# Edge features multiplied as split fp32r halves on 128 rows, with ScalarE filling the banks of all edge pairs and b_e added on TensorE or in DRAM

## What is computed

```python
ea = edge_attr @ w_e + b_e                     # (E, 64) @ (64, 256)
msg = relu(x[src] + ea)                        # gathered rows of x
agg = segment_sum(msg, dst, N)                 # dst is sorted
t = x + agg
h_local = bn(relu(t @ w1 + b1) @ w2 + b2 + x)
h_attn = bn(attention(x) @ out_w.T + out_b + x)    # 4 heads, blocks of 32 nodes
out = h_local + h_attn
out = out + relu(out @ m_w1 + m_b1) @ m_w2 + m_b2
result = layernorm(x + bn(out))
```

## Time and profile before

| | |
|---|---|
| time, median of 3 runs | 1360.22 us (1359.91 to 1360.58) |
| the profiled execution, its own time | 1364.96 us |
| its span, first to last instruction | 1363.1 us |
| PE busy | 1270.4 us, 93% of the span |
| POOL busy | 987.6 us, 72% |
| DVE busy | 904.9 us, 66% |
| ACT busy | 751.6 us, 55% |
| mean granted TensorE clock | 0.979 of 2.4 GHz |

### The profile page before, as it was taken

The page is one execution under the profiler, slowest core; times in us unless marked ns, Lnnn a source line. Parts: engine busy times, 40 slices in busy tenths (PEclk is TensorE's granted clock), DMA queues, the critical chain, the costliest instruction groups (busy, mean ns, idle before and its releaser), DMA issues.

```text
span 1363.1 us, 22611 instructions
## 1 busy us (share of the span) xinstructions
PE 1270.4 (93%) x8250; PEld 1024.2 (75%) x8250; DVE 904.9 (66%) x1763; ACT 751.6 (55%) x1617; POOL 987.6 (72%) x1032
## 2 busy tenths in 40 slices
PE   3787889999999999999999999999999999999997
PEld 2666678887877777777778777777877777778786
DVE  4988987666666665667666566666666666556652
ACT  1333335665665656566665666666656656565642
POOL 7777777777777777777777777777777777777710
PEclk6889999999999999999999999999999999999999
DMA  9777765555555554555555555555555555545511
GB/s 328 236 242 244 243 212 157 172 151 164 160 174 174 160 174 139 174 161 176 174 159 163 148 166 170 174 164 172 149 161 160 175 177 160 172 131 167 153 52 47
DMA packets 109648, 232.89 MB, mean 171 GB/s; under 512 B 21984, under 2 KB 46816, under 8 KB 109536
## 3 DMA queue, kind: packets, MB, share of 16 engines
q0 software_dynamic: 49152, 134.28, 34.1%
q1 hardware_dynamic: 58944, 93.87, 20.6%
q10 hardware_dynamic: 1440, 3.29, 0.6%
HBM read 206.19 MB, written 25.17 MB: 170 GB/s over the span
## 4 chain that ended last, share of the span: by engine, by line
POOL 35%; PE 23%; DMA 15%; issue 13%; ACT 7%; DVE 6%; SPq 0%; DVEq 0%; ACTq 0%
POOL xg L304 35%; DMA xg<-xb_dram,srcs 12%; PE both L677 8%; PE bank L722 4%; PE bank L707 4%; ACT bank L330 3%; PE bank L677 3%; ACT mh L334 2%; DVE onehot L545 1%; DMA aggT<-in_xT_dram 1%; DVE ml L533 1%; PE bank L731 1%; PE both L853 1%; DMA xg<-in_x_dram,srcs 1%; PE bank L800 1%
## 5 line engine op out<-in xcount | busy, mean ns | idle before, releaser
L304 POOL DMA_INDIRECT xg<-xb_dram,srcs x864 | 819.3, 948 | 263.2 <-issue 227.0
L330 ACT COPY bank<-xg 128x512 f32<-128x512 f32 x432 | 256.3, 598 | 373.5 <-DMA xg<-xb_dram,srcs 341.7
L533 DVE SCALAR_TENSOR_TENSOR ml<-bank,mh 128x512 fp32r<-128x512 f32 x512 | 328.6, 683 | 154.6 <-ACT mh L334 153.6
L334 ACT ACTIVATE mh<-bank 128x512 fp32r<-128x512 f32 x512 | 276.7, 593 | 137.6 <-PE bank L707 136.4
L707 PE MATMUL bank<-we,ea 64*128 64x256 f32 x2048 | 296.1, 409 | 56.7 <-DVE bank L442 28.3
L707 PEld LDWEIGHTS bank<-we,ea 64*128 64x128 f32 x2048 | 181.7, 191 | 139.1 <-issue 68.3
L722 PE MATMUL bank<-mh,onehot 128*128 128x256 f32 x1024 | 265.8, 297 | 8.3 <-DVE onehot L545 8.2
L722 PE MATMUL bank<-ml,onehot 128*128 128x256 f32 x1024 | 252.3, 284 | 0.0
L722 PEld LDWEIGHTS bank<-mh,onehot 128*128 128x128 f32 x1024 | 196.4, 192 | 51.8 <-issue 29.5
L304 POOL DMA_INDIRECT xg<-in_x_dram,srcs x160 | 167.3, 1046 | 50.8 <-issue 46.9
L722 PEld LDWEIGHTS bank<-ml,onehot 128*128 128x128 f32 x1024 | 197.1, 192 | 0.0
(11 more groups left out here) (100 smaller groups left out, 1368.3 us busy)
## 6 DMA issues: line engine op xcount, KB each, us to landing
ea<-in_ea_dram SPq DMA_DIRECT2D x128, 256.0 KB, 5.0
xg<-xb_dram,srcs POOLq DMA_INDIRECT x864, 3.0
xT<-in_xT_dram SPq DMA_DIRECT2D x32, 256.0 KB, 3.2
aggT<-in_xT_dram SPq DMA_DIRECT2D x32, 256.0 KB, 3.9
xrow<-in_x_dram SPq DMA_DIRECT2D x16, 512.0 KB, 6.1
xb_dram<-xrow SPq DMA_DIRECT2D x16, 512.0 KB, 3.7
oT_dram<-oT SPq DMA_DIRECT2D x32, 256.0 KB, 2.3
xn<-in_x_dram SPq DMA_DIRECT2D x32, 256.0 KB, 4.5
```

Of the source, the lines that this page charges most:

```text
L304: pool.indirect_dma_start(xg[:, q % NX, n * C:(n + 1) * C], None, t["x"] if q < XB_PAIR else k.xb_dram[:, :], bass.IndirectOffsetOnAxis(k. ...
L330: nc.scalar.copy(EA[q % 4][:, :], xg[:, q % NX, :]).then_inc(s_seed, 1)
L334: nc.scalar.activation(mh[:, q % NM, :], EA[q % 4][:, :], ACT.Relu).then_inc(s_mh, 1)
L533: nc.vector.scalar_tensor_tensor(ml[:, q % NM, :], EA[q % 4][:, :], 0.0, mh[:, q % NM, :].bitcast(fp32), ALU.max, ALU.subtract).then_inc(s ...
```

## The change

- The edge product. w_e is split into a rounded fp32r part `weh` and a remainder `wel`. The edge features of each group are split too: ACT rounds the whole tile into a PSUM bank (`round_ea`) and writes the rounded halves to SBUF (`high_ea`, two copies of 64 partitions), DVE writes the remainders (`low_ea`, two tensor_tensor of 64 partitions, one operand in PSUM). They are stacked: the 64 high rows and the 64 low rows of a pair fill 128 partitions of `eahl`. A tile is now two fp32r matmuls of 128 rows, one by `weh`, one by `wel`.
- The seed. ACT copies the gathered rows into the banks of all pairs. For the first 80 pairs PE adds b_e by one more fp32r matmul per tile (`be_ones` x `be_hl`). DVE seeds no more.
- `XB` is 32 in place of 16: parts of 256 KB, one per turn in place of one per two turns, and `XB_PAIR` is 80 as before.
- `round_ea` for a later group stands on ACT in odd turns behind `high` and ahead of `copy_agg`; it uses the bank of the turn's first pair and so waits until DVE's `low` of that pair is done. `high_ea` stands behind `copy_agg`. `low_ea` stands on DVE behind the two `low` of odd turns. The seed that takes that bank next waits for `low_ea`.
- For room in SBUF: `ea` has 2 buffers in place of 3, `xn` one in place of two, `ex` and `prob` share the place of `dif`, and `we` and the gammas lie in tiles that are used later.

```diff
-NEA = 3
+NEA = 2
-XB = 16
+XB = 32
-XB_PAIR = XB * PG + 16
+XB_PAIR = 2 * XB + 16
...
             def load_ea(n):
                 if n >= NEA:
-                    sp.wait_ge(s_prod, 2 * (n - NEA) + 2)
+                    sp.wait_ge(s_eah, n - NEA + 1)
+                    sp.wait_ge(s_eal, n - NEA + 1)
...
-                m = turn // 2
-                if turn % 2 == 1 and m < XB:
+                m = turn
+                if m < XB:
                     sp.wait_ge(s_xadd, m + 1)
                     sp.dma_start(xb_parts[m, :, :, :], k.xrow[:, m % 2, :, :]
                                  ).then_inc(s_xbst[m % 2], 16)
-                if turn % 2 == 1 and 2 <= m + 1 < XB:
+                if 2 <= m + 1 < XB:
                     load_part(m + 1)
...
-                        if j >= 2:
-                            sp.wait_ge(s_r, j - 1)
-                        sp.dma_start(k.xn[:, j % 2, :, :], x_blocks[j, :, :, :]
+                        if j >= 1:
+                            sp.wait_ge(s_r, j)
+                        sp.dma_start(k.xn[:, 0, :, :], x_blocks[j, :, :, :]
...
             def seed(q):
                 act.wait_ge(s_xg[q % NX], 32 * (q // NX + 1))
-                act.wait_ge(s_ml, q - 3)
+                if q < 4:
+                    act.wait_ge(s_set, 1)
+                else:
+                    act.wait_ge(s_ml, q - 3)
+                if q % 4 == 2 and 6 <= q and q // 4 + 2 <= NG:
+                    act.wait_ge(s_eal, q // 4 + 2)
                 nc.scalar.copy(EA[q % 4][:, :], xg[:, q % NX, :]).then_inc(s_seed, 1)
...
+            def round_ea(n, bank):
+                act.wait_ge(s_ea[n % NEA], 16 * (n // NEA + 1))
+                nc.scalar.copy(bank[:, :].bitcast(f32r), ea[:, n % NEA, :]).then_inc(s_eab, 1)
+
+            def high_ea(n):
+                nc.scalar.copy(eahl[0:ED, n % 2, 0, :], ea[0:ED, n % NEA, :])
+                nc.scalar.copy(eahl[ED:P, n % 2, 1, :], ea[ED:P, n % NEA, :]).then_inc(s_eah, 1)
...
                 for q in (a, b):
                     if q < NP:
                         high(q)
+                n = (turn + 3) // 2
+                if turn % 2 == 1 and n < NG:
+                    act.wait_ge(s_ml, a + 1)
+                    round_ea(n, EA[a % 4])
                 if turn % 2 == 1 and 3 <= turn <= 2 * NG + 1:
                     copy_agg(turn // 2 - 1)
-                n = turn // 2 + 1
-                if turn % 2 == 0 and EA_PE <= n < NG:
-                    act.wait_ge(s_ea[n % NEA], 16 * (n // NEA + 1))
+                if turn % 2 == 1 and n < NG:
+                    high_ea(n)
...
+            def low_ea(n, bank):
+                dve.wait_ge(s_eab, n + 1)
+                nc.vector.tensor_tensor(eahl[ED:P, n % 2, 0, :], ea[0:ED, n % NEA, :],
+                                        bank[0:ED, :], ALU.subtract)
+                nc.vector.tensor_tensor(eahl[0:ED, n % 2, 1, :], ea[ED:P, n % NEA, :],
+                                        bank[ED:P, :], ALU.subtract).then_inc(s_eal, 1)
...
-                for q in (a + 2, b + 2):
-                    if q < XB_PAIR:
-                        seed(q)
                 n = turn // 2
                 if turn % 2 == 0 and n >= 1:
                     if 2 <= n < NG + 2:
                         add_agg(n - 2)
-                    if n < XB:
-                        add_be(n)
                     if n < NG:
                         make_onehot(n)
+                if 1 <= turn < XB:
+                    add_be(turn)
                 for q in (a, b):
                     if q < NP:
                         low(q)
+                if turn % 2 == 1 and (turn + 3) // 2 < NG:
+                    low_ea((turn + 3) // 2, EA[a % 4])
...
-                for two in range(2):
-                    for pair in range(2):
-                        rows = slice(pair * ED, (pair + 1) * ED)
+                pe.wait_ge(s_seed, 2 * d + 2)
+                for pair in range(2):
+                    for two in range(2):
                         at = (2 * h + two) * P
-                        ins = nc.tensor.matmul(EA[(2 * d + pair) % 4][:, two * C:(two + 1) * C],
-                                               ea[rows, n % NEA, at:at + P], k.we[rows, :],
-                                               start=False, stop=True,
-                                               skip_group_check=True)
+                        if 2 * d + pair < XB_PAIR:
+                            nc.tensor.matmul(EA[(2 * d + pair) % 4][:, two * C:(two + 1) * C],
+                                             k.be_ones[:, :], k.be_hl[:, :], start=False, stop=True,
+                                             skip_group_check=True)
+                        for half in (k.weh, k.wel):
+                            ins = nc.tensor.matmul(EA[(2 * d + pair) % 4][:, two * C:(two + 1) * C],
+                                                   eahl[:, n % 2, pair, at:at + P], half[:, :],
+                                                   start=False, stop=True, skip_group_check=True)
                 ins.then_inc(s_prod, 1)
```

More of the change, by code:

```diff
@@ L48 @@
 TURNS = LAST_START + NODE_TURNS
-EA_PE = XB_PAIR // PG + 1
 def nodes_in(turn):
@@ L95, in gnn_layer @@
         k.rel = sb("rel", [P, NG, TG])
-        k.we = sb("we", [P, C])
-        k.be_rows = sb("be_rows", [P, C])
+        k.weh, k.wel = sb("weh", [P, C], f32r), sb("wel", [P, C], f32r)
+        k.be_rows, k.be_hl = sb("be_rows", [P, C]), sb("be_hl", [P, C], f32r)
+        k.be_ones = sb("be_ones", [P, P], f32r)
         k.xrow = sb("xrow", [P, 2, XB_ROWS, C])
@@ L160, in program @@
         s_oh = sem("s_onehot_made")
+        s_weh, s_wel = sem("s_we_high"), sem("s_we_low")
+        s_eab, s_eah, s_eal = (sem(n) for n in ("s_ea_high_in_bank", "s_ea_high", "s_ea_low"))
         s_pre = [sem(f"s_agg_preloaded_{n}") for n in range(2)]
@@ L236, in _ @@
                 i, p = turn // TI, turn % TI
-                if turn % 2 == 1 and turn // 2 + 2 < NG:
-                    load_ea(turn // 2 + 2)
-                m = turn // 2
-                if turn % 2 == 1 and m < XB:
+                if turn == 0:
+                    load_ea(2)
+                if turn % 2 == 0 and turn // 2 + 3 < NG:
+                    load_ea(turn // 2 + 3)
+                m = turn
+                if m < XB:
                     sp.wait_ge(s_xadd, m + 1)
@@ L297, in _ @@
                         pool.wait_ge(s_xbst[n], 16 * (XB // 2))
[L298 to L301 removed]
+                if q >= NX:
+                    pool.wait_ge(s_seed, q - NX + 1)
                 for n in range(2):
@@ L401, in node @@
                                          ).then_inc(s_root, 1)
+            act.wait_ge(s_we, 16)
+            nc.scalar.copy(k.weh[:, :], k.we[:, :]).then_inc(s_weh, 1)
+            for n in range(2):
+                round_ea(n, X[1 + n])
+                high_ea(n)
+                if n == 0:
+                    seed(0)
+                    seed(1)
             for turn in range(TURNS):
@@ L405, in _ @@
                 for q in (a + 2, b + 2):
-                    if XB_PAIR <= q < NP:
+                    if q < NP:
                         seed(q)
@@ L453, in _ @@
             dve.wait_ge(s_ber, 16)
-            seed(0)
-            seed(1)
+            step_of(nc.vector.tensor_scalar(k.be_hl[:, :], k.be_rows[:, :], 0.0, None, ALU.mult))
+            settle()
+            for row in (0, 32):
+                nc.vector.tensor_scalar(k.be_ones[row:row + 1, :], ident[row:row + 1, :], 0.0, 1.0,
+                                        ALU.mult, ALU.add)
+            step_of(nc.vector.tensor_copy(k.be_hl[0:1, :], k.be_rows[0:1, :]))
+            settle()
+            nc.vector.tensor_tensor(k.be_hl[32:33, :], k.be_rows[0:1, :],
+                                    k.be_hl[0:1, :].bitcast(fp32), ALU.subtract).then_inc(s_be, 1)
+            dve.wait_ge(s_weh, 1)
+            nc.vector.tensor_tensor(k.wel[:, :], k.we[:, :], k.weh[:, :].bitcast(fp32),
+                                    ALU.subtract).then_inc(s_wel, 1)
+            low_ea(0, X[1])
             dve.wait_ge(s_dstg, 16)
@@ L643, in node @@
                     ins.then_inc(s_y, 1)
+            low_ea(1, X[2])
             add_be(0)
@@ L690, in _ @@
                                 ).then_inc(s_baseT, 1)
-            pe.wait_ge(s_we, 16)
+            pe.wait_ge(s_be, 1)
+            pe.wait_ge(s_wel, 1)
             def products(d):
                 n, h = d // 2, d % 2
-                if h == 0 and n < EA_PE:
-                    pe.wait_ge(s_ea[n % NEA], 16 * (n // NEA + 1))
-                if 2 * d < XB_PAIR:
-                    pe.wait_ge(s_seedv, 2 * d + 2)
-                else:
-                    pe.wait_ge(s_seed, 2 * d + 2 - XB_PAIR)
-                for two in range(2):
-                    for pair in range(2):
-                        rows = slice(pair * ED, (pair + 1) * ED)
-                        at = (2 * h + two) * P
```

(13 more changed lines are left out.)

37 lines of the change are left out of this document (12 added, 25 removed).

## The result

The changed kernel takes **1368.07 us** (median of 4 runs, 1366.38 to 1369.74). The kernel before took 1360.31 in the same session (4 runs, 1359.91 to 1360.58). The ratio is 1.0057, 95% interval 1.0040 to 1.0075: 7.8 us slower. I had forecast slower, but by 28 us.

What follows compares the result with a forecast made beforehand. POOL bounds the kernel at 40.1 us a block, PE 1.4 behind; PE's new block of 41.2 takes over: 26 x 1.1 = +28.6, tail about -1, start 0, so +28 on 1360.2 gives 1388, range 1350 to 1402.

Steps and rivals of the forecast that it cites:

- a block of 41.2 us: PE's steady block of 8 turns: 38.67 + 0.8 product + 1.0 and 0.7 waits, against 40.1 before.
- the shorter gathers: POOL's first 160 gathers, no longer lengthened by DVE's seeds: 11 us saved, bounds 8 and 15.
- The product: Edge product on PE: new form costs +0.1 us a turn, +0.8 a block, bounds 0 and 1.6.
- My row of 0.96: Old product's eight 64-row instructions on PE, from their first start at 705.13 to the next work at 706.09.
- The two waits: PE waits in turns 0 and 2 of each steady block, forecast at 1.0 and 0.7 us.
- Turn 0: PE's transposes wait for copy_agg, queued on ACT behind round_ea, which waits for DVE's low: 1.0 us a block.
- Turn 2: PE waits for h2, delayed by ACT's and DVE's added steps: 0.7 us a block, bounds 0 and 1.2.
- Rival 1: POOL stays the bound and only its first phase counts: 1351 us (1348 to 1354), chance 0.24.
- Turn 40 starts when it did before: End of the start phase: PE's lag eats most of POOL's 11 us gain; bounds -8 and +6.
- Rival 3: Load loop of x + b_e parts, one per turn, slows the first turns: +51 us, 1438 in all, chance 0.05.
- a lag of 7 us: Turns 17 to 39: with b_e matmuls PE's block is 43.3 against POOL's 41, so PE falls some 7 us behind.
- SP's other steps: Edge loads with two buffers and the xn load with one, issued two or more turns ahead: costed at nothing.

Runs made afterwards that it cites:

- fp32_rows64_x_2: Changed kernel with the next x load issued early, the edge product in old 64-row fp32 form and a call's b_e matmuls first: 1387.93 us, ratio 1.0192.
- x_ahead: Changed kernel with SP issuing the load of the next part of x before the wait for this part's add: 1352.88 us, ratio 0.9941.
- both: Changed kernel with the next x load issued before the wait for the add, and copy_agg ahead of round_ea on ACT: 1350.52 us, ratio 0.9926.
- old_parts32_2: Kernel before with only the parts of x + b_e changed, to 32 of 256 KB, one per turn: 1368.26 us, ratio 1.0059.

## Why the prediction was right or wrong

**The direction was right by luck.** I had PE as the new bound of the steady part at a block of 41.2 us, and nothing in the start. The start eats what the shorter gathers save, and PE's own block is 39.71, less than POOL's 40.1. PE does set the pace of the changed kernel's steady part, but only because it comes late into it and catches up.

**The product: the step that failed most.** In the sum for a block I took +0.8 us. It is 7 x (1.17 - 1.37) + 0.18 = -1.2: from the start of the matmul before the group to the next group it is 1.17 us in the new form and 1.37 in the old, in six turns of eight, and 1.07 and 1.27 in turn 3. The prediction measured the old group from its own first start (1.06, 0.96), and so left out what lies ahead of it. The starts of single instructions in the trace of fp32_rows64_x_2 show it, and those of the kernel before have the same steps: 709.70 for the last dense matmul, 710.01 for the first of 64 rows, a gap of 0.31 where the dense ones follow each other at 0.22, another 0.32 to the second pair, and again 0.31 at the end (710.77 to 711.08). The 128-row form starts 0.03 after the dense one, and its one long step is the next, 0.31 (702.89 to 703.19). My row of 0.96 was the one turn of eight in which 64-row score matmuls run before the product: there the rows don't change on the way in, the start follows 0.11 us after, and there the new form is 0.18 longer. The price of 0.119 for one of the new matmuls was right (703.90 - 703.19 over six of them). The Trainium skill ("TensorEngine Tiling (Array Packing)", Key Properties) says that a change of the tiling mode, not of the tile alone, drains TensorE. The trace agrees so far as the starts come late, 0.31 at each change of rows and 0.11 where there is none. What the prediction cites from the Trainium skill for the old form ("TensorE: Matmul & The Clock Gate", Part 3), that small tiles in distinct row groups run side by side, the trace bears out too, with pairs of starts 0.007 us apart. But four steps of 0.22 gain only 0.07 us on eight fp32r matmuls at 0.119, and entering and leaving cost more than that.

**The two waits: right in place and cause, small in size.** Turn 0: forecast 1.0 (0.5 to 1.3), measured 1.14 by the row at 722.46. Turn 2: forecast 0.7 (0 to 1.2), measured 1.3, over its bound. The copies of 64x512 took 0.62 where I had 0.55. With a floor of 38.67 - 1.2 = 37.5 and 2.4 us of waits PE's block would be 39.9; the trace has 39.7. Of the 0.2 left over I know one source: the group behind the product gains too, since in `sum_group` the second matmul starts 0.12 us after the first, where it was 0.23. My 41.2 was wrong by the product (2.0 too much), less the waits (0.7 too little). With the old product PE's own block is 40.83 = 38.67 + 2.2: there the two waits alone make PE the bound, as forecast.

**Rival 1 and its condition.** It decides if product and waits together cost less than 1.4 us a block. I had 2.5 and gave it 0.24; they cost 39.71 - 38.67 = 1.0. So the condition held, but its time, 1351, needs a PE that starts in time, and the changed kernel missed it through the load loop: x_ahead takes 1352.9, both 1350.5.

**The start: the second step that failed.** "Turn 40 starts when it did before" had bounds of -8 and +6, and it was +11.5 in the profiled executions. Rival 3 named the loop, at a chance of 0.05, and put the landing at which it decides at 4.4 us, since the first 40 turns took 5.45 us each. Its parts were close: an add of 0.65 for 0.69, 0.4 for the issues, a landing of about 4 for 4.3. But the comparison was with the old pace. With gathers of 0.97 + 0.3 us POOL's turn would be 5.1, and the loop costs what lies between that and 5.6: 0.5 x 30 = 15 us, which is what x_ahead gave back. The shorter gathers were as forecast, 11 us and (1046 - 973) x 160 = 11.7 by the page, and were lost in the loop. They aren't its only cause: in old_parts32_2, where DVE seeds as before, the same loop takes 5.8 us and costs 7.9, so it was over the old pace as well. b_e on PE, which I had as the cause of a lag of 7 us, caused none in this kernel (turn 40 at 243.8 with it, 244.8 without).

**SP's other steps were costed at nothing.** For the edge loads that was right: the 171.1 us that ACT stood idle ahead of `round_ea` are all put down to DVE's `low`, none to an edge load.

## What to carry to other kernels

Price a group of matmuls from the start of the instruction before it to the start of the one behind it, in each of the places in which it stands: here a change between 64 and 128 rows was paid at both ends, outside the group. When a step gets faster, compare every loop beside it with the new pace, not the old. Look at blocks one by one before you take their mean: equal blocks told that PE had arrears, unequal ones that it waited for gathers. And a loop that loads, waits for a use and stores should ask for the next load ahead of the wait: one line moved turned this change from 0.6% slower to 0.6% faster.

## What the runs showed of the hardware that I had not expected

A change between fp32r matmuls of 128 rows and fp32 ones of 64 rows is dear when it comes often: one matmul of b_e and two instructions of a product in turn took 0.94 us a round (261.72 to 262.66), where a 128-row fp32r one takes 0.12 in a sequence of its kind and two 64-row fp32 ones side by side 0.22. Which part of it is the rows and which the type was not separated.
